# A fused LoRA and mixture-of-experts feed-forward kernel: the first weight transfer in two pieces, two transfers on ScalarE's queue, warm-up matmuls on another constant

## The reference

```python
c = x @ W + (x @ lora_A[itok]) @ lora_B[itok]            # 512 -> 512
result = c @ W_base.T + b_base
probs = softmax(c @ W_gate.T); top_p, top_i = top_k(probs, 2)   # renormalised
delta = ((c @ A.T) * route_w) @ B                         # 8 experts, rank 16
out = x + result + delta
```

## Time and profile before

| | us |
|---|---|
| median of 3 executions | 69.65 (69.59, 69.65, 70.81) |
| the profiled execution, its own time | 69.46 |
| its span | 67.8 |
| PE busy, of the span | 63.6 (94%) |
| PEld busy | 54.2 |
| DVE busy | 33.2 |
| ACT busy | 26.2 |
| POOL busy | 10.3 |

### The profile page before, as it was taken

How to read it: one execution, slowest core, us unless ns; L and a number is a source line. 1 busy time by engine, 2 the same in 40 slices (tenths; PEclk the granted TensorE clock), 3 DMA queues, 4 the chain that set the end, 5 groups by cost and what they waited for, 6 DMA issues and landing times.

```text
span 67.8 us, 1120 instructions
## 1 busy us (share of the span) xinstructions
PE 63.6 (94%) x340; PEld 54.2 (80%) x340; DVE 33.2 (49%) x126; ACT 26.2 (39%) x69; POOL 10.3 (15%) x30
## 2 busy tenths in 40 slices
PE   3999999999999999999999999999999999999920
PEld 3988898888888898888988988988988988988700
DVE  0034887000991799368517638428428428128100
ACT  4272873004972566123045324324324321321430
POOL 1000998703093001010010010010010000000000
PEclk9999999999999999999999999999999999999999
DMA  0899999996000056552004040040040040040044
GB/s 0 251 292 347 393 372 409 406 403 230 4 21 4 12 135 141 121 130 49 0 5 155 0 155 10 0 155 0 0 155 5 0 155 0 0 155 0 10 154 156
DMA packets 4648, 8.45 MB, mean 125 GB/s; under 512 B 793, under 2 KB 1049, under 8 KB 4642
## 3 DMA queue, kind: packets, MB, share of 16 engines
q1 hardware_dynamic: 4178, 7.70, 33.7%
q0 software_dynamic: 320, 0.54, 2.1%
q10 hardware_dynamic: 144, 0.13, 0.6%
HBM read 5.26 MB, written 2.10 MB: 109 GB/s over the span
## 4 chain that ended last, share of the span: by engine, by line
PE 94%; ACT 1%; issue 0%; DVE 0%
PE bank L426 17%; PE bank L428 16%; PE bank L427 16%; PE bank L450 12%; PE bank L434 7%; PE bank L512 5%; PE bank L505 4%; PE bank L518 4%; PE bank L515 4%; PE bank L486 3%; PE bank L526 2%; PE bank L472 1%; PE bank L493 1%; ACT y_out L290 1%; PE bank L482 1%
## 5 line engine op out<-in xcount | busy, mean ns | idle before, releaser
L426 PE MATMUL bank<-c_hi,x_hi 128*128 128x512 f32 x32 | 14.2, 443 | 0.0
L428 PE MATMUL bank<-c_hi,x_lo 128*128 128x512 f32 x32 | 12.6, 393 | 0.0
L427 PE MATMUL bank<-c_lo,x_hi 128*128 128x512 f32 x32 | 12.6, 392 | 0.0
L450 PEld LDWEIGHTS bank<-c_gh,x_raw 128*128 128x128 f32 x64 | 9.1, 189 | 0.7
L450 PE MATMUL bank<-c_gh,x_raw 128*128 128x152 f32 x64 | 9.6, 292 | 0.0
L428 PEld LDWEIGHTS bank<-c_hi,x_lo 128*128 128x128 f32 x32 | 6.0, 188 | 1.3
L290 ACT COPY y_out<-bank 128x512 f32<-128x512 f32 (+1 forms) x9 | 4.8, 541 | 5.4 <-PE bank L428 5.4
L426 PEld LDWEIGHTS bank<-c_hi,x_hi 128*128 128x128 f32 x32 | 6.0, 189 | 0.8
L241 POOL COPY c_gh<-lora_raw 128x64 f32<-128x64 f32 x8 | 2.5, 317 | 27.0 <-PE bank L450 27.0
L296 ACT CAST xa_t<-bank 128x128 fp32r<-128x128 f32 x8 | 2.1, 266 | 11.6 <-PE bank L472 11.5
L427 PEld LDWEIGHTS bank<-c_lo,x_hi 128*128 128x128 f32 x32 | 6.1, 190 | 0.5
(11 more groups left out here) (79 smaller groups left out, 105.0 us busy)
## 6 DMA issues: line engine op xcount, KB each, us to landing
x_raw<-x_t SPq DMA_DIRECT2D x8, 256.0 KB, 7.3
out<-y_out SPq DMA_DIRECT2D x7, 256.0 KB, 2.0
w_raw<-fold_in SPq DMA_DIRECT2D x4, 324.0 KB, 4.8
w_raw<-fold_in SPq DMA_DIRECT2D x4, 256.0 KB, 5.0
bw_rows<-bw_hi SPq DMA_DIRECT2D x8, 81.0 KB, 2.1
lora_raw<-lora POOLq DMA_DIRECT2D x8, 64.0 KB, 5.1
bw_rows<-bw_lo SPq DMA_DIRECT2D x4, 81.0 KB, 2.1
ffn_b_raw<-ffn_b SPq DMA_DIRECT2D x1, 256.0 KB, 8.3
```

The lines of the kernel that those rows point to most:

```text
L426: nc.tensor.matmul(out, a_hi, b_hi, start=first, stop=False)
L427: nc.tensor.matmul(out, a_hi, b_lo, start=False, stop=False)
L428: return nc.tensor.matmul(out, a_lo, b_hi, start=False, stop=last)
L450: mm = nc.tensor.matmul(g_bank[n][:, own_cols(t)], x_raw[:, t, c, :], c_gh[:, c, own_cols(t)], start=(c == 0), stop=(c == KC - 1), skip_gr ...
```

## The change

There are four edits.

1. SP's first transfer, wa of chunk 0 (648 columns), becomes two: the last 128 columns of W^T with gh (264 columns, 132 KB, new semaphore `w_first_loaded`), then the other 384 columns (192 KB, `wa_loaded[0]`). `fold_gh` takes its four column blocks in the order 3, 0, 1, 2, so that its first matmul of chunk 0 needs only the first piece.
2. wb of chunks 0 and 1 are issued by ScalarE's queue, ahead of all else that ScalarE does. SP issues wb of chunks 2 and 3 as before.
3. ScalarE waits for `w_first_loaded` and then for `wa_loaded[0]` before its first copy.
4. The warm-up matmuls read a constant (bfloat16 ones) that the framework fills before the kernel starts. The tile of zeros, its memset on VectorE and the semaphore are gone.

```diff
+FIRST = D - P
-        zeros = sb("zeros", [P, P // 2])
+        w_first_loaded = sem("w_first_loaded")
-        zeros_ready = sem("zeros_ready")
...
+        def load_wb(engine, m):
+            engine.dma_start(w_raw[:, m, D + GH:], fold_in[m, :, D + GH:]).then_inc(wb_loaded[m], DMA)
+
         @block.sync
         def _(sp):
-            def load_fold(m):
+            sp.dma_start(w_raw[:, 0, FIRST:D + GH], fold_in[0, :, FIRST:D + GH]).then_inc(w_first_loaded, DMA)
+            sp.dma_start(w_raw[:, 0, 0:FIRST], fold_in[0, :, 0:FIRST]).then_inc(wa_loaded[0], DMA)
+            for m in range(1, KC):
                 sp.dma_start(w_raw[:, m, 0:D + GH], fold_in[m, :, 0:D + GH]).then_inc(wa_loaded[m], DMA)
-                sp.dma_start(w_raw[:, m, D + GH:], fold_in[m, :, D + GH:]).then_inc(wb_loaded[m], DMA)
-
-            for m in range(KC):
-                load_fold(m)
+                if m >= 2:
+                    load_wb(sp, m)
...
         @block.scalar
         def _(act):
+            for m in range(2):
+                load_wb(act, m)
+            act.wait_ge(w_first_loaded, DMA)
             for m in range(KC):
                 act.wait_ge(wa_loaded[m], DMA)
...
         @block.vector
         def _(dve):
-            nc.vector.memset(zeros[:], 0.0).then_inc(zeros_ready, 1)
...
             def fold_gh(m):
-                pe.wait_ge(wa_loaded[m], DMA)
-                for i in range(KC):
-
+                pe.wait_ge(w_first_loaded if m == 0 else wa_loaded[m], DMA)
+                for i in (3, 0, 1, 2):
+                    if m == 0 and i == 0:
+                        pe.wait_ge(wa_loaded[0], DMA)
...
-            pe.wait_ge(zeros_ready, 1)
+            ones = nc.const_aps.tensor(1.0, [P, P], mybir.dt.bfloat16)
             for _ in range(WARM_UPS):
-                nc.tensor.matmul(bwgh_bank[:, 0:P], zeros[:].bitcast(mybir.dt.bfloat16), zeros[:].bitcast(mybir.dt.bfloat16),
+                nc.tensor.matmul(bwgh_bank[:, 0:P], ones, ones,
                                  start=True, stop=True)
```

## The result

| kernel | median us | range | executions |
|---|---|---|---|
| before | 69.59 | 69.3 to 70.81 | 6 |
| changed | 72.97 | 71.85 to 73.8 | 6 |

The change makes the kernel slower: ratio 1.0422, 95% interval 1.0362 to 1.0482. The profiled execution took 73.09 us, 3.63 more than the 69.46 before; its span is 71.4.

What follows compares the result with a forecast made beforehand. The prediction took TensorE to bound the kernel, busy 63.6 of 67.8 us, with delays after 3.81 paid unless the adapters' wait swallows them. 69.46 + 0.60 (late wb_hi) + 1.63 (late rate rise) = 71.7 us, range 69.7 to 72.9.

Steps and rivals of the forecast that it cites:

- case (B): The forecast itself: late wb_hi +0.60 and late rate rise +1.63 give 71.7 us, own range 71.1 to 73.0; chance 0.50.
- The memset: Start of the kernel: without the memset PE starts at about 0.9 instead of 1.13, which wins nothing by itself.
- The first piece: The 132 KB piece on SP's queue, issued at 0.88, lands at 3.0 to 3.3 us, when the warm-ups end.
- T: Landing time of wa's second piece in chunk 0: taken as 4.4 us, bounds 3.78 and 6.37.
- The load behind the wait: ScalarE's table load, covered before, now waits for wa_loaded[0]: 1.28 us plus 0.02, with wb_hi done at T + 2.62.
- rival D: The table load also has an unseen drain of about 1.38 us: 73.1 with case (B), 71.4 with Rival A; chance 0.04.
- Rival C: Not slower: the table load begins before wa_loaded[0] lands and costs nothing, 69.35 us; chance 0.07.
- The late wb_hi: Chunk 0's wb_hi ends at 7.02 instead of 5.10; L515 starts at 8.04 instead of 7.33, 0.71 later, +0.60 net.
- SP's queue: Tiles of x issued about 0.46 us earlier, adapters within half a microsecond of 16.20; term taken as zero.
- The rate: TensorE's rise from 1.2 to 2.4 GHz, before at about 7.07, comes a run of 3.26 us after 7.12: +1.63 us.
- Rival A: The holes in PE's work don't hold the rate back; the change costs only +0.60, 70.1 us; chance 0.36.
- The hole at the adapters: PE's wait before L526, 0.11 us of "issue" at 17.58, absorbs that much of the 0.71 delay, leaving +0.60.

Runs made afterwards that it cites:

- e4: Changed kernel with all nine weight transfers on SP's queue, the split and the table load behind the wait kept: 69.30 us, ratio 0.9988 to the kernel before.
- e6: Changed kernel with all weight transfers on SP's queue and a tiny copy first on ScalarE, so the table load runs early: 68.79 us, ratio 0.9893.
- e7: Kernel of e6 with SP waiting for the adapters before it issues the third tile of x: 69.11 us, ratio 0.9875 to the kernel before.
- e2: Kernel before, with ScalarE waiting twice for wa_loaded[0] so the table load stands behind the first wait: 69.58 us, ratio 1.003.
- e12: Changed kernel with 10 idle matmuls ahead of L512 of chunk 0, the first hole left open: 71.08 us, ratio 1.0258 to the kernel before.
- e3: Changed kernel with 12 idle matmuls ahead of the wait for the second piece and 10 ahead of L512: 70.81 us, ratio 1.022 to the kernel before.
- e9: Changed kernel with a tiny copy ahead of ScalarE's waits and wb of chunk 1 back on SP's queue: 69.54 us, ratio 1.0023 to the kernel before.

## Why the prediction was right, and where its sizes were off

The direction, the mechanism and the likeliest case (B) held. The median of 72.97 lies 1.3 above the forecast of 71.7, just past the range's edge of 72.9; 69.6 times the ratio gives 72.5. Against the profiled execution, +3.63 was measured and +2.23 summed.

- **The memset:** right. PE starts at 0.88 and wins nothing by it.
- **The first piece:** wrong, 3.7 instead of 3.0 to 3.3. It came early (3.0 to 3.1) only where ScalarE's queue was silent (e4, e6, e7).
- **T:** mis-sized, 4.4 against 5.53. The step that was wrong is that the two queues have carried 580 KB when the piece lands. It left out wb of chunk 1, ScalarE's second transfer, and let the queues share by bytes where they share by packets. By 5.53 us SP's queue had moved 0.61 MB and ScalarE's 0.52. Even before the change 0.57 MB had moved when the first 324 KB landed, so the bytes asked for up to a piece never gave its landing.
- **The load behind the wait:** right, 1.28 us and 0.02 behind it. The trace refutes rival D: no tail follows the load. The steps behind T were 2.50 us instead of 2.62, since back-to-back copies start 0.52 apart. Rival C fell with the order of the program.
- **The late wb_hi:** with T as measured, four L517 at the higher rate would end at 8.19 + 0.92 = 9.11, where L515 had started at 7.33. That is 1.78, against 0.71.
- **SP's queue:** the term of zero held, its reason did not. The first tile of `x` was issued at 5.17, not 0.46 earlier than 5.19, and the copy of the adapters started at 17.16 instead of 16.20, outside the bound of half a microsecond. TensorE came later still, at 21.29.
- **The rate:** the kind was right, the size 2.2 against 1.63: chunk 1 starts 12.91 - 8.92 = 3.99 later, and 3.99 - 1.78 = 2.21. My "run of 3.26 us" was a guess at a regularity, and that its size came near is luck. Over the runs here the higher rate begins anywhere from between 4 and 5 us (e2, e12) to over 12, so it has to be treated as a spread. Rival A is refuted by e3: with the late `wb_hi` alone the cost is 1.3 us between the medians, and the changed kernel's six executions all lay above that kernel's four.
- **The hole at the adapters:** 0.11 in the sum, 3.99 - 3.63 = 0.36 in fact. The chain's "issue" of 0.11 rests on modelled ends of matmuls; the 0.28 of PEld in the earlier trace rows was nearer.

## What to carry to other kernels

An instruction that the framework inserts takes the place that the waits leave it: two waits ahead of an engine's first operation can put a 1.3 us table load on the critical path, and a tiny operation ahead of them keeps it off. A transfer on a second queue is not added to the first but shared with it (up to 3.78 us the engines moved 0.57 MB before the change and 0.58 after it), so whatever the first matmul needs belongs alone at the front. Here cutting it in pieces beside a busy second queue made it later, since its packets shrank and its share of the bytes with them. Then look next at what holds the end of the stage (here the adapters), since in e9 a gain ahead of it was worth nothing until that moved. Where an early hole can't be avoided, idle matmuls in it are cheap, and here they were worth about 2 us, a part of which was an earlier landing.

## What was not expected of the hardware

- The moment at which TensorE's higher rate began differed by about 8 us between kernels that all begin with 24 warm-ups, and the clock column shows 1.00 before the first rise, so only the spacing of the loads tells.
- The split and the second queue each by itself delay the last of wa by 0.0 to 0.6 us, and together by 1.0 to 1.75 (3.78 to 4.8 to 5.53), because queues share by packets and not by bytes.
- A 132 KB piece landed no sooner than a 324 KB transfer (3.7 against 3.8 us) once another queue was active.
